# Starting the ball block's filling six steps earlier, with a step between each pair of engines

## What is computed

```python
x = x + _L0_attn_ref(_L0_cond_ref(x, cond_1024, ...), Wq, Wk, Wv, betas, Wo)
x = x + _L0_ffn_ref(_L0_cond2_ref(x, cond_1024[:, None, :], ...), ...)
```

## Time and profile before

| | us |
|---|---|
| median of 3 runs | 3677.01 (3676.51 to 3677.66) |
| the profiled execution, its own time | 3681.4 |
| its span, first to last instruction | 3679.6 |
| PE busy | 3405.7 (93%) |
| DVE busy | 2207.2 (60%) |
| ACT busy | 1698.4 (46%) |
| POOL busy | 383.3 (10%) |

### The profile page before, as it was taken

How to read it: one execution, slowest core, us unless ns; L and a number is a source line. 1 busy time by engine, 2 the same in 40 slices (tenths; PEclk the granted TensorE clock), 3 DMA queues, 4 the chain that set the end, 5 groups by cost and what they waited for, 6 DMA issues and landing times. The chain is left out here.

```text
span 3679.6 us, 51595 instructions
## 1 busy us (share of the span) xinstructions
PE 3405.7 (93%) x18082; PEld 1915.6 (52%) x18082; DVE 2207.2 (60%) x6620; ACT 1698.4 (46%) x3271; POOL 383.3 (10%) x250
## 2 busy tenths in 40 slices
PE   8999999999996788998899758999999999999999
PEld 3455555555554333444444435555555555555554
DVE  3243343343357567778775648777777777777773
ACT  2233333333342455555556325555555555555552
POOL 0000000000000001111211211111111111111110
PEclk8999999999998799999999879999999999999999
DMA  4110120110000200000000030000000000000000
GB/s 175 53 61 32 35 72 32 35 61 32 29 15 13 76 5 8 7 15 14 11 12 12 9 131 21 20 21 21 21 21 21 21 27 21 26 27 27 21 27 20
DMA packets 77985, 120.47 MB, mean 33 GB/s; under 512 B 10224, under 2 KB 66315, under 8 KB 72608
## 3 DMA queue, kind: packets, MB, share of 16 engines
q1 hardware_dynamic: 77728, 117.17, 9.4%
HBM read 96.13 MB, written 16.83 MB: 31 GB/s over the span
## 5 line engine op out<-in xcount | busy, mean ns | idle before, releaser
L2616 PE MATMUL wps<-w_wqkv,w_hT 128*128 128x512 f32 x768 | 379.2, 618 | 3.1 <-DMA w_wo<-in_wwo 3.1
L2654 PE MATMUL wps<-w_xnT,w_w 128*128 128x512 f32 (+1 forms) x768 | 352.5, 599 | 24.5 <-DVE w_xnT L2479 20.3
L2238 POOL TENSOR_TENSOR w_rn<-w_n,w_mhalf 128x16 f32<-128x16 f32 x64 | 187.3, 2926 | 1097.7 <-DVE w_n L2416 1097.7
L2266 ACT ACTIVATE w_pr<-w_sm,w_nmx,w_rn 128x256 f32<-128x256 f32 (+1 forms) x512 | 286.5, 562 | 10.0 <-DVE w_nmx L2397 9.4
L1217 POOL TENSOR_TENSOR b_routs<-b_rins,b_expo 128x4 f32<-128x4 f32 x88 | 89.8, 1023 | 1839.0 <-DVE b_rins L1405 1839.0
L2654 PEld LDWEIGHTS wps<-w_xnT,w_w 128*128 128x128 f32 (+1 forms) x768 | 133.6, 179 | 217.9 <-issue 194.3
L656 PE MATMUL ps<-xT,b_late 128*128 128x512 f32 x512 | 245.8, 602 | 0.0
L672 PE MATMUL ps<-hid,b_late 128*128 128x512 f32 x512 | 240.8, 592 | 0.0
L1250 ACT ACTIVATE bb_pr<-ps 128x1024 f32<-128x1024 f32 x128 | 130.6, 1020 | 198.6 <-PE ps L1793 197.7
L2253 ACT ACTIVATE w_pT<-wps 128x512 f32<-128x512 f32 (+1 forms) x128 | 69.6, 544 | 329.7 <-PE wps L2563 329.7
L2616 PEld LDWEIGHTS wps<-w_wqkv,w_hT 128*128 128x128 f32 x768 | 138.2, 193 | 132.8 <-issue 127.8
(11 more groups left out here) (329 smaller groups left out, 6680.4 us busy)
## 6 DMA issues: line engine op xcount, KB each, us to landing
b_late<-in_ew SPq DMA_DIRECT2D x32, 1024.0 KB, 6.7
w_xa<-xs SPq DMA_DIRECT2D x16, 512.0 KB, 3.9
w_xin<-xs SPq DMA_DIRECT2D x64, 128.0 KB, 3.8
xT<-in_xT SPq DMA_DIRECT2D x8, 512.0 KB, 3.8
xres<-in_x SPq DMA_DIRECT2D x32, 128.0 KB, 2.2
x<-x1t SPq DMA_DIRECT2D x32, 128.0 KB, 1.7
b_mod<-ada SPq DMA_DIRECT2D x16, 256.0 KB, 3.2
xs<-bb_wb SPq DMA_DIRECT2D x8, 512.0 KB, 2.9
```

Source lines behind the costliest of these rows:

```text
L2238: g.tensor_tensor(rn[:, i % 2, t], n2[:, n % 2, 1], mhalf[:], ALU.pow).then_inc(nr_ok, 1)
L2266: ins = a.activation(pr[:, j, lo:], sm[:, j, lo:], ACT.Exp, bias=nmx[:, G % 2, j:j + 1], scale=rn[:, i % 2, t, h:h + 1], accum_out=rs[:, G ...
L2616: ins = te.matmul(to, hT[:, i % 2, k, t * P:(t + 1) * P], wqkv[:, i // B, k, s * 512:(s + 1) * 512], start=(k == 0), stop=(k == KD - 1))
L2654: ins = te.matmul(to[0:n], w1[:, i // B, k, lo:lo + n], xnT[:, k], start=(k == 0), stop=(k == KD - 1))
```

## The change

Three things are changed.

First, `AHEAD` goes from `J * B - 3` to `J * B - 9`. Each ball step from -31 to -2 is run six steps earlier, so g = G - 214: g = -31 now falls on step 183, g = -21 (the first turned rows) on step 193, g = -2 on step 212. POOL's clearing goes to step 195.

Second, for the first four ball tiles (q = 0 to 3, all in the filling) a tile's work is spread over more steps: DVE's `projected` stands at +2 in place of +1, `ask_heads` at +3 in place of +2, PE's `turn_heads` at +6 in place of +7. ACT's squares stay at +2 and the taking away of queries and keys at +7. Later tiles stay as they were.

Third, `u` gets memory of its own, since it is now written from step 187 on, while the expert weights are still in use, and `acc`, a buffer of the ball block's feed-forward, moves to where `u` was.

```diff
-        AHEAD = J * B - 3
+        AHEAD = J * B - 9
...
             for G in STEPS:
-                if G == J * B + 2:
+                if G == AHEAD + 12:
                     pool.wait_ge(o_mm, B * J)
...
-    u = late[:, 3 * half + 2 * NH * W:4 * half].rearrange("p (t d) -> p t d", d=D)
+    u = keep("u", [P, NT, D])
...
-        acc = sb("acc", [P, L])
+        acc = late[:, 3 * half + 2 * NH * W:3 * half + 2 * NH * W + L]
...
+    def tile_at(G, first, later):
+
+        q = tile_due(G, first)
+        if q is not None and q < NT:
+            return q
+        q = tile_due(G, later)
+        return q if q is not None and q >= NT else None
+
...
-        if tile_due(G, 7) is not None:
-            yield "zq", tile_due(G, 7)
-            yield "zk", tile_due(G, 7)
+        if tile_at(G, 6, 7) is not None:
+            yield "zq", tile_at(G, 6, 7)
+            yield "zk", tile_at(G, 6, 7)
...
-            if tile_due(G, 1) is not None:
-                projected(tile_due(G, 1))
+            if tile_at(G, 2, 1) is not None:
+                projected(tile_at(G, 2, 1))
...
-            if tile_due(G, 2) is not None:
-                ask_heads(tile_due(G, 2))
+            if tile_at(G, 3, 2) is not None:
+                ask_heads(tile_at(G, 3, 2))
...
-            if tile_due(G, 7) is not None:
-                turn_heads(tile_due(G, 7))
+            if tile_at(G, 6, 7) is not None:
+                turn_heads(tile_at(G, 6, 7))
```

More of the change, by code:

```diff
@@ L1224, in squares_summed @@
                     filled(pool, "fn", b - 1)
-                g.tensor_copy(acc[:], fsq[:, 0]).then_inc(acc_ok, 1)
+                g.tensor_copy(acc, fsq[:, 0]).then_inc(acc_ok, 1)
             else:
                 pool.wait_ge(acc_ok, n)
-                g.tensor_tensor(acc[:], acc[:], fsq[:, m % 2], ALU.add).then_inc(acc_ok, 1)
+                g.tensor_tensor(acc, acc, fsq[:, m % 2], ALU.add).then_inc(acc_ok, 1)
         def step(G):
```

## The result

The change makes the kernel faster by a third of a per cent: 3664.9 us (median of 8 runs, 3660.4 to 3671.5) against 3677.3 us for the kernel before (median of 8 runs beside them, 3672.8 to 3682.3). The ratio is 0.9968, with a 95% interval of 0.9957 to 0.9980, so 7 to 16 us, with 12.4 between the medians. The profiled execution took 3667.9 us, its span is 3666.1.

The account below looks back on a forecast made before the run. The tail was taken as a chain across engines, stretched by the filling on DVE. Walk -7.4, seam -1.2 and last projection -1 gave -9.6 us, rounded to -10: 3667.0 us from the median 3677.0, range 3661 to 3675.

Parts of the forecast that it names:

- The cover under the expert products: Filling steps -31 to -22, moved beside PE's expert products, were costed at nothing, PE's work hiding them.
- the seam: Ahead of tile 28's queries: column work of steps -29 and -28 no longer precedes x1t; -1.2 us.
- Stretch 1: Queries of tile 28 to L772 of tile 28: 17.6 us before, 22.8 forecast (+5.2).
- Stretch 2: L772 of tile 28 to L741 of tile 29: 19.1 us forecast, DVE filling it without a break.
- Stretch 4: L772 of tile 29 to L741 of tile 30: 18.0 us before, 14.2 forecast (-3.8).
- Stretch 7: L772 of tile 31 to L809 of tile 31: 12.9 us before, 8.6 forecast (-4.3).
- Stretch 3: L741 to L772 of tile 29: 19.8 us before, 24.8 forecast (+5.0), as `ask_heads` no longer covers ACT's chain.
- The wait for the bank: In stretch 2, PE's turned heads wait some 3 us until DVE takes the projection from their bank; costed at nothing.
- Half eaten: Rival, chance 0.25: low clock also covers tiles 28 and 30, `ask_heads` sticks out more; gain only 3.6 us, 3673.4.
- cover fails: Rival, chance 0.05: under the expert products, DVE's weighting and ACT's gelu queue behind the filling; +7 and 1, 3685 us.
- nothing: Rival, chance 0.03: the tail's pace comes from elsewhere and the change does nothing; 3677 us.
- The rival of the high clock: Rival, chance 0.15: with shorter tail waits TensorE stays at 2.4 GHz, 5 us more gained over two periods; 3662 us.

Follow-up runs that it names:

- pe_kept_busy: The change with 29 spare 128x512 products added on PE where it waits in the tail, results not used: 3656.4 us, ratio 0.9949 to the kernel before.
- tile2_early: The change, but `projected` and `ask_heads` of ball tile 2 one step earlier, at +1 and +2 as before: 3661.0 us, ratio 0.9958 to the kernel before.
- proj_first: The change, but for ball tiles 0 to 3 DVE's copies of the projection stand ahead of the expert column's work: one run of 3664.4 us.
- buffers_only: The kernel before with only `u` and `acc` moved as in the change, no filling step moved: 3676.1 us, ratio 1.0000.

## Why the prediction was right, and where it was not

The forecast was 3667.0 in a range of 3661 to 3675; 3664.9 was measured. By its steps:

- **The cover under the expert products** held: L772 of tile 27 has 0.18 us of issue ahead of it in place of a wait of 1.19 for DVE, PE is busy for 33.82 of the 34 us ahead of 1056, and the seam is 15.6 us in place of 16.8, the forecast 1.2.
- **The walk.** 124.0 us was forecast from tile 28's queries to L809 of tile 31, 124.1 and 124.3 were measured. The sum is closer than its terms. Stretch 1 was 1.4 too long: it started from a measured stretch with the queries at 3.36 us, and they took 2.02. Stretch 2 was 1.3 too short: I took the clock as high at its start, and L772 and the transposes behind it took 1.14 and 1.97 us, after a wait of 2.55. Stretch 4 was 1.3 too long: PE worked through it without a break, as foreseen, but its work took 12.9 us. Stretch 7 was 2.2 too short, all of it the clock, since pe_kept_busy did it in 7.6 us: the memory read at 1.14 and the values at 3.67 us, beside 0.70 and 2.00 in pe_kept_busy. Three of these four misses are the level of the clock in one piece, and together the seven cancel: a sum that came out right by more luck than its terms deserve. Two of the sums are also added up loosely: the terms given for stretches 1 and 5 make about 23.1 and 13.3 us, not 22.8 and 13.0. And of the signs named, L772 of tile 28 came 2.6 us later than before, not 4, and that of tile 31 at 1202.80, not 1205.
- **Stretch 3**, where the change was said to hurt, took 24.1 us for 24.8. tile2_early puts that mechanism at 4.8 us, where the prediction had +5.0. The wait of L772 behind it was the longest, as foreseen, at 8.41 us for some 10. It is the largest thing left to mend inside the change.
- **The wait for the bank** ahead of tile 29's queries came as foreseen (3.62 us, released by `projected`), and cost next to nothing: without most of it the way to L809 is 0.3 to 0.5 us shorter (proj_first).
- **The last projection** stayed at 3.78 us; the 1 us taken for it did not come.
- **The waits of DVE for the ball block's projection**, 3.78 us in the earlier trace rows, are gone, and nothing waits for L1865 in the tail.
- **Half eaten, cover fails, nothing** did not come. The low clock that the first of these speaks of did stand over stretch 7 and the last projection, for 3.2 us of the forecast, and stretches 1, 3 and 4 came out as much shorter.
- **The rival of the high clock** was mis-sized, though it was not the one that happened. It put the low clock's price at 5 us over two long waits. pe_kept_busy measured 10.1 us of tail (9.3 against the change's second profile): the last pieces (values, last projection, first ball products) stood at the low level too, with waits of only 2.7 and 2.2 us near them. TensorE: Matmul & The Clock Gate in the Trainium skill (What's actually happening), by which activity releases the throttle, is borne out by both kernels with spare products, as far as the granted clock of 0.96 to 0.99 shows it.
- **Not in the sum at all**: some 1.5 us at the ball block's beginning, which the prediction put at nothing because no step is moved there, and the differences between executions of one program. The forecast took the stretches of one profiled execution as the kernel's; that this execution took 4.4 us more than the median was a sign that it might not be typical.

## What to carry to other kernels

Where engines take turns and TensorE waits a few microseconds each time, price the clock as a term of its own, piece by piece, from the two lengths that the same row has in the trace; here it was as large as the whole gain of reordering the work, and a line of useless products in PE's idle time brought it without moving anything. Splitting a step between engines pays where its second half waited for the first, but look at whom the old order covered: work that stood in front of another engine's wait was free, and behind it is bare. Before two spans are compared, profile the old kernel twice: here its two spans were 9.1 us apart.

## What the runs showed of the hardware that was not expected

- The idle time ahead does not settle the level by itself. After the same wait of 2.55 us for DVE L772 of tile 28 took 1.14 us in the change and 0.70 in proj_first; after the same wait of 1.56 us tile 28's queries took 3.36 and 3.64 us in the two profiles of the kernel before and 2.02 in buffers_only. What does settle it was not found here.
- Executions of one program differ by whole pieces at the low level: 6.50 or 3.70 us for 16 products at about 1915 us, at an order and waits that are the same. In the first 56 us, between two profiles of the kernel before, rows such as L701 at 3.05 or 1.98 us made 2.9 us.
- 32 spare products, some 28 us of PE's work, made the kernel before 14.7 us faster (3677.1 to 3662.4), PE's busy time in 1090 to 1210 us rising from 80.5 to 104.1 us.
